# Two cross-attention stages: the first context, the first norm and a tile's closing chain moved

## The reference, cut to what matters

```python
x = x + tanh(g_xattn[0]) * _L0_xattn_ref(layernorm(x), ctx, ctx)            # stage one
...
x = x + tanh(g_xattn[2]) * _L2_xattn_ref(layernorm(x), ctx, mask, wq, ...)  # stage three
...
def _mha(q, k, v):                                # stage one: no projections
    scores = einsum('bhqd,bhkd->bhqk', qh, kh) / sqrt(hd)   # then a causal mask
    out = einsum('bhqk,bhkd->bhqd', softmax(scores), vh)
...
def _L2_xattn_ref(x, cond, mask, wq, bq, ...):    # stage three
    q = _w8a8_linear(x, wq, bq)                   # rows and weights rounded to +-127
    k, v = cond @ wk.T + bk, cond @ wv.T + bv
    o = softmax(q @ k.T * inv_sqrt_d + mask) @ v
    return _w8a8_linear(o, wo, bo)                # o's rows rounded again: a row's
                                                  # largest |value| / 127 is its scale
```

## Time and profile before

| | us |
|---|---|
| median of 3 runs (lowest, highest) | 4793.55 (4791.98, 4799.23) |
| the profiled execution | 4788.1 |
| its span, first to last instruction | 4786.3 |
| TensorE busy in the span | 4039.2 (84%) |
| VectorE / ScalarE / GpSimd busy | 2614.7 / 2007.9 / 1614.0 |
| stage one | about 8.9 to 507 |
| stage three | about 2009 to 2860 |

### The profile page before, as it was taken

One profiled execution on the slowest core, in us unless ns is written; L12 is line 12 of the kernel. 1 busy time (PEld: TensorE's weight loads), 2 busy tenths in 40 slices (PEclk: granted clock), 3 DMA queues, 4 the chain that ended last, 5 costly groups with the idle time before them and its releaser, 6 DMA issues. The chain is left out here.

```text
span 4786.3 us, 79212 instructions
## 1 busy us (share of the span) xinstructions
PE 4039.2 (84%) x30154; PEld 3351.4 (70%) x30154; DVE 2614.7 (55%) x5937; ACT 2007.9 (42%) x3334; POOL 1614.0 (34%) x1130
## 2 busy tenths in 40 slices
PE   6999359996868799779988876689999999999977
PEld 5777248885756644367777764379999999999963
DVE  5787554446757511256676654545555555555542
ACT  5788223332212211146666552334444444445421
POOL 3333013332212122111111100655566556556521
PEclk9999669997989899879999998889999999999988
DMA  4333025530000033021111111601011011001002
GB/s 126 107 105 92 26 88 170 161 87 1 1 1 1 25 102 91 27 71 44 49 46 38 52 49 32 157 27 31 27 31 32 23 31 36 23 27 31 27 1 70
DMA packets 168188, 259.26 MB, mean 54 GB/s; under 512 B 75916, under 2 KB 141644, under 8 KB 159036
## 3 DMA queue, kind: packets, MB, share of 16 engines
q1 hardware_dynamic: 167820, 254.25, 17.8%
HBM read 236.25 MB, written 17.98 MB: 53 GB/s over the span
## 5 line engine op out<-in xcount | busy, mean ns | idle before, releaser
L692 DVE CUSTOM_DVE_ANT_0 xh_soft<-xh_s,xh_mask 128x500 f32<-128x500 f32 x768 | 487.1, 675 | 114.9 <-PE xh_s L604 109.0
L614 PE MATMUL xh_t<-tables,xh_soft 128*125 128x128 f32 x3072 | 421.2, 290 | 23.1 <-ACT xh_probsT L856 14.7
L614 PEld LDWEIGHTS xh_t<-tables,xh_soft 128*125 128x125 f32 x3072 | 379.9, 196 | 81.6 <-issue 42.2
L876 POOL TENSOR_TENSOR xh_ctx_low<-xh_ctxT,xh_ctx_high 128x1000 fp32r<-128x1000 f32 x96 | 223.8, 2349 | 560.9 <-ACT xh_ctx_high L836 557.2
L856 ACT ACTIVATE xh_probsT<-xh_t 125x512 f32<-125x512 f32 x640 | 340.2, 598 | 172.4 <-PE xh_t L614 171.9
L849 ACT ACTIVATE xh_soft<-xh_soft,xh_neg_max 128x1500 f32<-128x1500 f32 x256 | 393.2, 1542 | 23.9 <-DVE xh_neg_max L700 23.9
L1343 DVE CUSTOM_DVE_ANT_0 xg_soft<-xg_s,xgw_mask 128x500 f32<-128x500 f32 x384 | 246.5, 677 | 284.2 <-PE xg_s L1253 283.4
L1442 POOL TENSOR_TENSOR xg_soft<-xg_soft,xg_recip 128x1500 f32<-128x1500 f32 x128 | 344.0, 2687 | 10.0
L1397 ACT ACTIVATE xg_soft<-xg_soft,xg_neg_max 128x1500 f32<-128x1500 f32 x128 | 198.1, 1548 | 333.1 <-DVE xg_neg_max L1347 333.1
L1277 PE MATMUL xg_o<-xg_probsT,xg_values 125*128 125x224 f32 x1536 | 303.0, 354 | 6.2 <-ACT xg_probsT L1404 5.2
L1277 PEld LDWEIGHTS xg_o<-xg_probsT,xg_values 125*128 125x128 f32 x1536 | 287.2, 191 | 7.2 <-ACT xg_probsT L1404 5.6
(11 more groups left out here) (483 smaller groups left out, 10508.8 us busy)
## 6 DMA issues: line engine op xcount, KB each, us to landing
xh_ctxT<-ctxT SPq DMA_DIRECT2D x32, 1500.0 KB, 7.4
xh_values<-ctx SPq DMA_DIRECT2D x16, 1500.0 KB
x_ctxT<-ctxT SPq DMA_DIRECT2D x16, 1500.0 KB, 22.3
x_ctx_rows<-ctx SPq DMA_DIRECT2D x16, 1500.0 KB
xgw_raw<-ctxT SPq DMA_DIRECT2D x48, 500.0 KB, 4.0
f1b_weight<-f_weights SPq DMA_DIRECT2D x32, 448.0 KB, 4.5
xh_mask<-mask_BxSxS_ff SPq DMA_DIRECT2D x32, 328.1 KB
f1b_wgu<-f_wgu SPq DMA_DIRECT2D x33, 256.0 KB, 2.7
```

The source lines that it names most:

```text
L614: mm = pe.transpose(bank[0:KC, i * 128:(i + 1) * 128], soft[m % 8][:, n * KC:(n + 1) * KC], ident)
L692: v.tensor_tensor_reduce(soft[m % 8][:, j * THIRD:(j + 1) * THIRD], bank[:, 0:THIRD], add, 1.0, -3.0e38, ALU.add, ALU.max, tops[g % 2][:, ...
L876: g.tensor_tensor(ctx_low[b % copies][:, :, cols], ctxT[:, :, cols], whole(ctx_high[b % copies][:, :, cols]), ALU.subtract).then_inc(s["lo ...
```

## The change

It has four parts. (1) The first context's load is issued in the setup block, in stage three behind the two large weight loads, and the setup of stage three ends without waiting for the scales to have come back (that wait is VectorE's now, at the first `Q2`). The setup's semaphores are a set of its own. (2) `L` and `LE` of tile 0 stand ahead of the first context's `H` and `B`. (3) The first context's `H` runs on ACT and its `B` on VectorE in both stages, and consumers wait third by third. (4) The closing chain of stage three is cut: `Y` ends with the bias, the scale (`YB`) follows the first two score entries of the next group, the rounding (`YC`) the third, ahead of the fourth.

```diff
-    plan = [("H", (0, j)) for j in range(3)] + [("B", (0, j)) for j in range(3)] + [("L", 0), ("LE", 0)]
+    plan = [("L", 0), ("LE", 0)] + [("H", (0, j)) for j in range(3)] + [("B", (0, j)) for j in range(3)]
...
-            plan += scores(0, 0) + context + scores(0, 1) + soft("E", 0) + weigh(0) + front(2, "L") + [("V", (g // 2, 0, 3))] * even
-            plan += soft("E", 1) + soft("E", 2) + weigh(1) + scores(1, 0) + scores(1, 1) + back(2, "Y2") + front(3, "Q") + weigh(2)
+            plan += scores(0, 0) + context + scores(0, 1) + back(2, "YB") + soft("E", 0) + weigh(0) + front(2, "L") + [("V", (g // 2, 0, 3))] * even
+            plan += soft("E", 1) + soft("E", 2) + weigh(1) + scores(1, 0) + back(2, "YC") + scores(1, 1) + back(2, "Y2") + front(3, "Q") + weigh(2)
...
+                    if kind == 0:
+                        sy.dma_start(ctxT[:, :, :], w["ctxT"][0]).then_inc(s["ctx_in"], 16)
                     if kind == 2:
...
                             load(wkvT[:, i, :, :], w[name].rearrange("(k p) n -> p k n", p=128))
+                        sy.dma_start(ctxT[:, :, :], w["ctxT"][0]).then_inc(s["ctx_in"], 16)
                         load(bq_all[:, :], every_row(w["bq"]))
...
                         sy.dma_start(so_all[:, :], every_row(w["scales"][D:2 * D])).then_inc(s["stored"], 16)
-                        sy.wait_ge(s["stored"], 48)
...
-                sy.dma_start(ctxT[:, :, :], w["ctxT"][0]).then_inc(s["ctx_in"], 16)
                 rest(0)
                 rest(1)
                 context_here(0)
...
                 def make_keys(b, h):
-                    pe.wait_ge(s["low_done"], 3 * b + 3)
                     for j in range(3):
+                        pe.wait_ge(s["low_done"], 3 * b + j + 1)
...
                     elif op == "Y2":
-                        pe.wait_ge(s["q_ready"], quantised["Y", at])
+                        pe.wait_ge(s["q_ready"], quantised["YC", at])
...
+                    elif op == "B" and m[0] == 0:
+                        cols = slice(m[1] * THIRD, (m[1] + 1) * THIRD)
+                        v.wait_ge(s["high_done"], m[1] + 1)
+                        v.tensor_tensor(ctx_low[0][:, :, cols], ctxT[:, :, cols], whole(ctx_high[0][:, :, cols]),
+                                        ALU.subtract).then_inc(s["low_done"], 1)
...
                     elif op == "Q2":
+                        if m == 0:
+                            v.wait_ge(s["stored"], 48)
...
-                            quantise_vector(v, s, step, row[:, :], row[:, :], xq[:, :], scale[:, 0:1], inv[:, 0:1])
+                    elif op == "YB":
+                        quantise_scale(v, s, step, row[:, :], scale[:, 0:1], inv[:, 0:1])
+                    elif op == "YC":
+                        quantise_round(v, s, step, row[:, :], row[:, :], xq[:, :], inv[:, 0:1])
```

More of the change, by code:

```diff
@@ L255, in quantise_vector @@
     v.tensor_scalar(q, scratch, -127.0, None, ALU.max).then_inc(s["q_ready"], 1)
+def quantise_vector(v, s, step, src, scratch, q, scale, inv):
+    quantise_scale(v, s, step, src, scale, inv)
+    quantise_round(v, s, step, src, scratch, q, inv)
 class Banks:
@@ L358, in heads_plan @@
     if kind == 2:
-        plan += [("Y2", PAIRS - 1), ("Y3", PAIRS - 1)]
+        plan += [(op, PAIRS - 1) for op in ("YB", "YC", "Y2", "Y3")]
     return plan
@@ L367, in head_attention @@
         st = Stage(nc, ctx, f"xh{kind}",
-                   "load padded scales_done stored v w_ready w_high here high_done low_done q_high q_low keys_high "
+                   "stored v here high_done low_done q_high q_low keys_high "
                    "var_ready rstd_ready xn_ready q_ready q_rows neg_max exp_done weighed oT_ready divided added "
@@ L423, in head_attention @@
                 sb.number(({"Y": "o", "Y2": "oqT", "Y3": "y"}[op], at))
-        quantised = {key: n + 1 for n, key in enumerate(key for key in plan if key[0] in ("LE", "Y"))}
+        quantised = {key: n + 1 for n, key in enumerate(key for key in plan if key[0] in ("LE", "YC"))}
         with ExitStack() as setup:
+            before = Stage(nc, setup, f"xw{kind}", "load w_ready padded filled copied q_ready v scales_done w_high low_done")
+            b = before.sem
             if kind == 2:
@@ L440, in load @@
                         n += 1
-                        sy.dma_start(dst, src).then_inc(s["load"], 16)
+                        sy.dma_start(dst, src).then_inc(b["load"], 16)
+                    if kind == 0:
+                        sy.dma_start(ctxT[:, :, :], w["ctxT"][0]).then_inc(s["ctx_in"], 16)
                     if kind == 2:
@@ L452, in _ @@
                         load(bv_all[:, :], every_row(w["bv"]))
-                    sy.wait_ge(s["load"], 16 * n)
+                    sy.wait_ge(b["load"], 16 * n)
                     if kind == 2:
-                        sy.wait_ge(s["scales_done"], 1)
+                        sy.wait_ge(b["scales_done"], 1)
                         sy.dma_start(w["scales"].rearrange("(k p) -> p k", p=128), w_scale[:, :],
@@ L490, in _ @@
                         for i in range(4):
[L491 removed]
+                            pe.wait_ge(b["q_ready"], i + 1)
                             if i:
[L493 to L494 removed]
+                                pe.wait_ge(b["copied"], i)
+                            transpose_pair(pe, view, w_int, core.ident_bf[:, :]).then_inc(b["filled"], 1)
                     @block.scalar
@@ L499, in _ @@
                         for i in range(4):
-                            a.wait_ge(s["filled_s0"], i + 1)
+                            a.wait_ge(b["filled"], i + 1)
                             a.activation((wqT, woT)[i // 2][:, :, (i % 2) * 128:(i % 2 + 1) * 128], view,
-                                         ACT.Copy).then_inc(s["copied_s0"], 1)
-                        a.wait_ge(s["load"], 16 * 7)
-                        a.activation(wkvT_high[:, :, :, :], wkvT[:, :, :, :], ACT.Copy).then_inc(s["w_high"], 1)
-            st.reset()
+                                         ACT.Copy).then_inc(b["copied"], 1)
+                        a.wait_ge(b["load"], 16 * 7)
+                        a.activation(wkvT_high[:, :, :, :], wkvT[:, :, :, :], ACT.Copy).then_inc(b["w_high"], 1)
+            before.reset()
         soft = [st.sb(f"soft{i}", [128, SK]) for i in range(8)]
@@ L587, in scores @@
                         pe.wait_ge(s["q_low"], 2 * u + 2)
-                    if j == 0 and pair == 0 and half == 0 and kind == 0:
-                        pe.wait_ge(s["low_done"], 3 * b + 3)
+                    if pair == 0 and half == 0 and kind == 0:
+                        pe.wait_ge(s["low_done"], 3 * b + j + 1)
                     if j == 0 and pair == 0 and half == 0 and kind == 2:
@@ L828, in _ @@
                                          scale=c[:, C_PAIR + h:C_PAIR + h + 1]).then_inc(s["q_high"], 1)
-                    elif op == "H" and kind == 2:
+                    elif op == "H" and (kind == 2 or m[0] == 0):
                         b, cols = m[0], slice(m[1] * THIRD, (m[1] + 1) * THIRD)
@@ L865, in _ @@
                         layernorm_pool(g, s, ln, core.minus_half, m)
-                    elif op == "H" and kind == 0:
+                    elif op == "H" and kind == 0 and m[0]:
                         b, cols = m[0], slice(m[1] * THIRD, (m[1] + 1) * THIRD)
@@ L872, in _ @@
                         g.tensor_copy(ctx_high[b % copies][:, :, cols], ctxT[:, :, cols]).then_inc(s["high_done"], 1)
-                    elif op == "B":
+                    elif op == "B" and m[0]:
                         b, cols = m[0], slice(m[1] * THIRD, (m[1] + 1) * THIRD)
```

30 lines of the change are left out of this document (15 added, 15 removed).

## The result

| | before | changed | ratio (95% interval) |
|---|---|---|---|
| first comparison, median us (lowest, highest) | 4792.76 (4791.37, 4799.23) | 4762.36 (4758.28, 4768.23) | 0.9935 (0.9918, 0.9952) |
| second comparison | 4787.15 (4778.02, 4796.65) | 4762.21 (4756.99, 4765.91) | 0.9947 (0.9933, 0.9961) |
| span of the profiled execution | 4786.3 | 4764.4 | |

The change makes the kernel 0.5 to 0.65% faster, 25 to 30 us. I had forecast 4788, with a range down to 4768. Single executions of either kernel lie up to 19 us apart, and the profiled one of the changed kernel was among its slower ones.

The account below looks back on a forecast made before the run. TensorE was taken to bound stages one and three once they run. The terms -7.0 - 16.5 + 3.1 + 14.7 = -5.7 us gave 4782.4 for the profiled execution and 4788 on the median, with an 8-in-10 range of 4768 to 4802.

Parts of the forecast that it names:

- Stage one's start: Stage one: first score product 10.3 us earlier, partly lost to POOL's late second context; -7.0 us, bounds 5 and 10.3.
- Stage three's start: Stage three: first key product at 2039.9 instead of 2056.41, TensorE not stopped again; -16.5 us.
- The chain's waits: Stage three's closing chain: wait at `V` goes, but `Y2` starts 0.44 us later in 7 tiles; +3.1 us.
- The clock: Closing chain: `Y2`'s 2.26 us idle time lowers TensorE's clock in 6 of 7 tiles, 2.4 us each; +14.7, bounds 0 and 35.4.
- that gap: TensorE idle times: clock stayed full after 0.99 and 0.83 us, but fell after stage one's 1.43 to 3.5 us.
- rival B: Closing chain: `Y2` waits but the clock does not fall; -20.4 us, 4773; chance 0.22.
- faster: Whole kernel: a measured time below 4784.0 us; chance given as 0.42.
- Rival C: Closing chain works as written, VectorE reaching the rounding before TensorE wants it; -30.5 us, 4763; chance 0.06.
- D: Closing chain: clock falls for 10.1 us in all 7 tiles, 5.05 each; +15.0 us, 4808.6, slower; chance 0.12.
- E: Both starts give little (-5 and -12), second context late, scales holding VectorE; with chain's +17.8, +1 us, 4794; chance 0.10.

Follow-up runs that it names:

- no_chain: Changed kernel with the closing chain in one piece again, scale and rounding at the end of `Y`; 4760.63 us, ratio 0.9951 to the kernel before.
- chain_only: Kernel before with only the closing chain cut in three steps, both starts as before; 4789.93 us, ratio 1.0001 to the kernel before.
- no_front1: Changed kernel with stage one's start as before; 4773.75 us, ratio 0.9971 to the kernel before.
- yc_late: Changed kernel with the rounding (`YC`) two score copies later, behind `scores(1, 1)`; 4789.02 us, ratio 1.0004 to the kernel before.
- le_early: Changed kernel with stage three's `LE` (layernorm's end and rounding) moved ahead of the keys; 4712.39 us, ratio 0.9843 to the kernel before.
- after: The changed kernel itself, in its first profiled execution, with no further edit; span 4764.4 us.
- le_yc_values: Changed kernel with `LE` ahead of the keys, rounding ahead of `scores(1, 0)`, second values' load behind stage one's second context load; 4693.36 us, ratio 0.9791 to the kernel before.
- again: The changed kernel run once more with no edit; 4762.21 us, ratio 0.9947 to the kernel before.

## Why the prediction was wrong

The forecast was -5.7 us, and the measured change is -25 to -30. By its own steps:

- **Stage one's start, -7.0**: first product at 21.36 for 21.2, right. POOL's cast of the second context at 46.69 for 45.5, so a little more was lost there. The 1 us that I took for a fall of the clock was too small: behind the place I had put the shift at 7, and the trace has 4.8, with a stretch at 1.2 GHz that the kernel before does not have. Undoing the part costs 11.5 us by medians, and 5.1 or 9.3 by traces. The size is right within what can be told, and the mechanism of the start itself.
- **Stage three's start, -16.5**: the key product came 16.4 us earlier, and undoing the part costs 19.5. Right. VectorE's wait for the scales held up nothing that showed: `Q2`'s first row was made at 2040.80, behind the subtractions.
- **The chain's waits, +3.1**: the wait at `V` gone, `Y2` waiting 2.25 and 0.44 later, as worked out. In sum it came to nothing, because less work fell into the next stretch at 1.2 GHz, behind `LE`: 43.4 us in seven tiles, where no_chain has 50.7, which gives back some 3.1. My sum had no term for a fall that already stood in each tile, and the same oversight is in the expectation of chain_only, which priced the shorter stretches at 1.5 each as if all of them lay behind the wait.
- **The clock, +14.7**: this is the step that failed. I said that an idle time of 2.26 us "is on the other side of that gap", and took a fall in six of seven tiles. It was one, worth some 1.5 us, and none in no_front1; taking the whole chain back moves the time by 1.6 us (no_chain), putting it alone into the kernel before by 1.0 (chain_only). The price of a fall was somewhat high (2.4 forecast; 1.9 in yc_late, 1.5 for the short ones in le_early). The rule was wrong: that length alone decides. The six cases in stage one, from 1.43 us, were all followed by falls, and I read from them a limit on the length. Stage one's own idle times do not bear it out when all fourteen traces are counted (60 to 495 us, those that begin at the full clock): of 47 between 1.4 and 2.3 us 13 have no stretch at 1.2 GHz within 4 us behind them, among them one of 2.24 us (no_chain, at 357.7: the clock is 1.00 from 350 to 366). All 39 between 2.3 and 3.7 us have one, and none of 71 between 0.8 and 1.2. My six were a small sample in which none happened to be spared. In stage three equal waits of 2.24 us went both ways within one kernel, the changed one and chain_only; the waits of 3.44 us were followed by a fall in all of seven, and those of 1.0 in none.

Without the clock term and with the chain at nothing the forecast's own terms give -23.5, that is 4770 on the median shown then, and -25 was measured in the larger comparison (-30 in the first). That is rival B with the chain's 3.1 taken out. I gave B 0.22, and the mechanism that I put first was one for which my rows had nothing of that length in that stage. (The chances named for "faster" add up to 0.43, not 0.42, which changes nothing.)

Rival C (nothing in the place of the removed wait) came near the time, 4763, and is wrong as a mechanism: the wait for the rounded rows is in the trace, 15.7 us in seven. D is not the change's course, but yc_late, 1.2 us per tile further, lands at the time of the kernel before. E did not happen.

## What to carry to other kernels

A stretch at 1.2 GHz behind an idle time is no fixed price per microsecond of idleness: the same wait costs its own length in one tile and 1.5 to 3 us more in another (3.4 or 6.8 us at the lower level, at the ratio of the earlier trace rows). Give such a term the whole range from none to all tiles as a case with two ends, and look at the falls that are already in each period, since they grow and shrink with a change beside them; of each count only what lies behind the wait's end. And where a chain is cut to free the start of a group, put each piece into a gap of its engine that the trace shows (here 1.08 us ahead of the second scores): the piece placed two copies later turned waits of 0.99 and 0.83 us into one of 2.25.

## What the runs showed of the hardware

- In stage three the granted clock fell behind TensorE waits of 2.24 to 2.26 us in 0, 1, 3 and 7 of 7 equal tiles in four kernels (no_front1, after, chain_only, le_early), behind 3.43 to 3.45 us in 7 of 7 (yc_late), and behind 0.8 to 1.0 us in none. The stretches at 1.2 GHz at `LE`'s wait of 6.3 us were of 6.8 or of 10.2 us; they began 0.9 to 4.3 us before the wait's end.
- VectorE's single-input instructions of 0.29 us took 2.3 us while POOL subtracted, one for one with POOL's instructions of 2.35, seven times in stage three. Moving `LE`, with them, to where POOL is idle was worth 50 us, twice what the whole change gave.
- VectorE's masked copies took 0.67 to 0.68 us beside the same POOL work in le_early and le_yc_values, no longer than alone.
- One program's executions lay 5 to 21 us apart (no_front1: 4770.37 to 4775.51; yc_late: 4779.59 to 4800.58). Two traces of one program, after and again, have stretches at 1.2 GHz in other places, and differ by 4.2 us at the end of stage one; one trace can't size a term of 5 us there.
